# Cross-attention layer on one core: queries turned by DMA and VectorE instead of TensorE, with new written orders

## The chip, the cores and the metric

The kernel runs on one NeuronCore of a Trainium2 chip. The metric is the device time of one execution in microseconds (us); less is better. A measurement of this kernel repeats within about 0.2%.

## What is computed

One transformer block with cross-attention, 16 batches, all in float32: 512 queries of width 256 against 1601 keys, 16 heads of width 16, and an MLP of width 1024.

```python
def _L0_xattn_ref(Q, KV, Wq, bq, Wk, bk, Wv, bv, Wo, bo, W1, b1, W2, b2, ln_q_g, ln_q_b, ln_ff_g, ln_ff_b):
    qn = _layer_norm(Q, ln_q_g, ln_q_b)
    q = (qn @ Wq + bq).reshape(B, Lq, H, DH).transpose(0, 2, 1, 3)
    k = (KV @ Wk + bk).reshape(B, Lkv, H, DH).transpose(0, 2, 1, 3)
    v = (KV @ Wv + bv).reshape(B, Lkv, H, DH).transpose(0, 2, 1, 3)
    scores = jnp.einsum('bhqd,bhkd->bhqk', q, k) / jnp.sqrt(jnp.float32(DH))
    attn = jax.nn.softmax(scores, axis=-1)
    ctx = jnp.einsum('bhqk,bhkd->bhqd', attn, v)
    ctx = ctx.transpose(0, 2, 1, 3).reshape(B, Lq, D)
    x = Q + (ctx @ Wo + bo)
    h = _layer_norm(x, ln_ff_g, ln_ff_b)
    ff = jax.nn.silu(h @ W1 + b1) @ W2 + b2
    return x + ff
```

## The kernel before

The batches run one after the other, and each batch in four quarters of four heads. A quarter q of batch b has 26 pairs of score products (L1324, letter `s`, one per head and half a tile of keys), 26 exponentials on ScalarE (L863, letter `e`), and 13 tiles of products of values with probabilities (L1343, `p`, four 32-column matmuls a tile; a four-byte matmul stands as two records). Softmax subtracts the exact row maximum: score rows with queries on the partitions (L1309, `rows_ps`, letter `m`, 52 a quarter) are made a quarter and more ahead, and VectorE reduces each (L1079, `chunk_max`). Every fourth group of rows holds the last 65 keys: four short matmuls of 65 columns. There are two buffers of `rows_ps`, so TensorE may be two `m` ahead of VectorE. The maxima, negated (letter `n`), go through a small TensorE product (`turn`, L1244), a ScalarE copy and three DMAs of SyncE (`place_shift`, L539) into the last rows of `q_stack`, before the next quarter's scores.

Scores and rows are products of bfloat16 parts: ScalarE writes a projection (`whole`, L824) and its first part (L828), GpSimd the second and third (L641 to L644), and SyncE copies the parts into `k_stack` and `q_stack` (`place`, L455; `repeat_parts`, L464).

All other matmuls are the letter `d`, one `side` bank for all of them: keys (`k`, L1250), values (`v`, L1258), query transposes (`x`, L1248), query projection (`q`, L1254), output projection (`wo`, L1262), transposes of the MLP's input (`h`, L1265), and the MLP (`w1`, L1269; `w2`, L1273). The list `BOTH` says which of them stand in which quarter; the output projection and MLP of batch b-1 and the keys, values and queries of b+1 stand in batch b. In the first and last batch those that have no batch to serve are left out, the letters stay.

The strings `TENSOR`, `SCALAR` and `VECTOR`, one a quarter, are the order on each engine, written out by hand: each letter is one step. They are the same for all 16 batches. SyncE and GpSimd follow their own `quarter` functions in order of the code, and wait there for semaphores; nothing behind a waiting instruction of a queue goes ahead.

The context arrives in chunks of 512 keys through `load_ctx` in blocks of 32 channels, so that VectorE's transpose of 32x32 blocks (`turn_ctx`, L1047, letter `t`) makes the channels-first form `ctxT` of it. The rows of `wk_sb` and `wv_sb` are permuted to fit (`load_rows`). `ctx_blocks` has two halves, used in turn by chunks 0 to 3. The queries go another way: `load_x` (L504) brings x as it is into `x_nat`, VectorE takes moments (`x` in `VECTOR`, in three stages), GpSimd normalises in place (`normalise_x`, L661), TensorE transposes (8 products of 128x128 in two steps), and ScalarE scales and shifts out of the bank into `qnT` (L799).

Of the kernel before, what the change touches and what calls it, by code (L numbers as in the profile page):

```python
# [35 lines left out]
P = 128  # L36
# [30 lines left out]
N_SECOND = 3 + KC * (P // 32)  # L67
# [12 lines left out]
def tiles_in(c):  # L80
# [25 lines left out]
    "pmmssssmddmdddssmmdddssssmmddddssmddmsddmsssmdmddmdmpppmssmsdsmdddmssmdddmsdmsssmddmpmmpmddddmsmsssm"  # L106
    "ddmmddsmsssmppsmmddsmddmsmsssmddddsmmsppdmmdddssssmdmdmssmdmssmsdsmmppp",
    "ssdssmmddmssmssmpmssmssmpmmsssspmdssssmmpppmsssmsmdssmmssdmssmssmdmmppmmssdmssmssmmdmdmmpmddsmssdddd"
    "mmpmddddsssmmdmdmmppsmddddsmssmddmdmddmdmsssmsddmmp",
    "pmmdssmdmssdmsmsdddmmssddmsmsssddmdmdddddmmssssddmdmdpppsmmsssdddmdmdddsdmmsssdmdmsddsmmppmmdssmssmd"  # L110
    "ddmssmddddmmsssdmsmdddmmppddmmssddmmsspppdmdddssmssmdmmssssmdssmmppmmss",
# [15 lines left out]


# [131 lines left out]
def xattn_kernel(nc, x, ctx, wq, bq, wk, bk, wv, bv, wo, bo, w1, b1, w2, b2, gq, cq, gf, cf, out):  # L260
    with ExitStack() as stack:
# [27 lines left out]
        ctx_blocks = sb("ctx_blocks", [P, 2, KC * CHUNK])  # L289
        ctxT = sb("ctxT", [P, KC, BLOCK * BLOCKS])  # L290
# [14 lines left out]
        probs = sb("probs", [P, PROBS, 4 * LQ])  # L305
        o_sb = sb("o_sb", [P, LQ])
# [72 lines left out]
        x_guessed = sem("x_guessed")  # L379
        h_guessed = sem("h_guessed")  # L380
# [1064 lines left out]
```

## Time and profile before

| | |
|---|---|
| median of 3 runs | 3350.74 us (3349.56 to 3351.97) |
| profiled execution | 3350.18 us |
| its span | 3348.4 us |
| TensorE clock granted, mean | 0.989 |
| TensorE / VectorE / ScalarE / GpSimd busy | 98% / 78% / 65% / 29% |

The quarters of a batch in the middle of the run last about 50.3, 49.5, 51.8 and 49.9 us. In this document a quarter of the trace is a stretch between the first TensorE rows of two of them: the second quarter of batch 6 is 1349.0 to 1398.7 us, and the last batch's four quarters begin at 3112.4, 3162.7, 3209.2 and 3257.5 and end at 3297.6. A row of a timeline gives start, length, engine, line, operation and tiles; neighbouring equal instructions are merged, and matmuls overlap in the pipe, so the time that a group takes from TensorE's stream is read from its start to the start of the next row. A row of windows gives the stretch and its length, then busy us and instructions of TensorE's matmuls, its weight loads, VectorE, ScalarE and GpSimd, then the granted clock, the DMA engines' share and GB/s.

### The profile page before, as it was taken

What the parts mean: (1) busy time and instruction counts of PE and PEld (TensorE: products, weight loads), DVE (VectorE), ACT (ScalarE), POOL (GpSimd) and SP (SyncE); (2) the same over time, 40 slices, a digit from 0 to 9 for tenths busy, and PEclk for the clock granted to TensorE, in tenths of its full rate; (3) what the DMA queues carried; (4) which work ended last, traced back from release to release, by engine and by line L of the source; (5) the groups of instructions that cost most, each with busy time, mean ns of one, the idle gap of its engine ahead of it and who ended that gap; (6) DMA issues with size and microseconds to landing.
All of it is one profiled execution on the core that took longest, in us unless ns stands there. A gap on an engine that the chain in (4) does not pass through costs nothing.

```text
span 3348.4 us, 51845 instructions
## 1 busy us (share of the span) xinstructions
PE 3273.7 (98%) x19204; PEld 1598.5 (48%) x19204; DVE 2598.7 (78%) x4771; ACT 2165.4 (65%) x2731; POOL 963.1 (29%) x1312
## 2 busy tenths in 40 slices
PE   6899999999999999999999999999999999999988
PEld 2344444554445455444554445455444554445435
DVE  5778778787887878778787887878778777887762
ACT  1466666666666766667666666766667666666654
POOL 5032324223332332324222332232324213342200
PEclk7899999999999999999999999999999999999998
DMA  5332222322223332222322223331222322222200
GB/s 106 66 54 42 42 48 46 59 53 45 48 42 51 60 59 38 42 51 48 59 53 40 48 46 52 60 59 36 41 52 51 59 53 37 49 45 43 47 7 13
DMA packets 201790, 162.94 MB, mean 49 GB/s; under 512 B 142912, under 2 KB 182848, under 8 KB 198464
## 3 DMA queue, kind: packets, MB, share of 16 engines
q1 hardware_dynamic: 199504, 158.79, 26.4%
q8 instruction: 152, 2.49, 0.3%
q10 hardware_dynamic: 2032, 0.82, 0.1%
q14 instruction: 102, 0.84, 0.1%
HBM read 46.43 MB, written 8.39 MB: 16 GB/s over the span
## 4 chain that ended last, share of the span: by engine, by line
PE 83%; SPq 10%; DVE 3%; DMA 2%; issue 1%; ACT 1%; ACTq 0%; DVEq 0%
PE o_ps L1343 20%; PE rows_ps L1309 19%; PE scores L1324 18%; SPq L455 6%; PE side L1273 6%; PE side L1250 5%; PE side L1269 5%; PE side L1258 4%; SPq L464 3%; DVE chunk_max L1079 2%; PE side L1254 2%; PE side L1262 1%; DMA x_nat<-in_x 1%; SPq L539 1%; PE side L1244 0%
## 5 line engine op out<-in xcount | busy, mean ns | idle before, releaser
L1079 DVE TENSOR_REDUCE chunk_max<-rows_ps 128x1 f32<-128x512 f32 (+1 forms) x3328 | 2109.3, 666 | 602.3 <-PE rows_ps L1309 586.5
L863 ACT ACTIVATE probs<-scores 128x1024 f32<-128x1024 f32 (+1 forms) x1664 | 1633.0, 1020 | 733.2 <-PE scores L1324 615.6
L1309 PE MATMUL rows_ps<-k_stack,q_stack 96*128 96x512 bf16 (+1 forms) x4096 | 1139.8, 337 | 35.9 <-DVE chunk_max L1079 22.0
L1324 PE MATMUL scores<-q_stack,k_stack 99*128 99x512 bf16 (+1 forms) x3328 | 991.0, 380 | 7.2 <-ACT probs L863 5.6
L1343 PE MATMUL o_ps<-probs,v_sb 128*32 128x512 f32 x6656 | 811.1, 602 | 0.2 <-ACT o_sb L852 0.2
L1309 PEld LDWEIGHTS rows_ps<-k_stack,q_stack 96*128 96x128 bf16 x4096 | 342.5, 97 | 675.9 <-DVE chunk_max L1079 438.1
L1324 PEld LDWEIGHTS scores<-q_stack,k_stack 99*128 99x128 bf16 (+1 forms) x3328 | 321.3, 99 | 372.9 <-issue 64.9
L1343 PEld LDWEIGHTS o_ps<-probs,v_sb 128*32 128x32 f32 x6656 | 171.0, 109 | 409.4 <-issue 348.0
L697 POOL TENSOR_TENSOR o_sb<-o_sb,denom 128x512 f32<-128x512 f32 x31 | 39.4, 1271 | 1086.3 <-DVE denom L1065 1086.3
L1269 PE MATMUL side<-hT,w_sb 128*128 128x256 f32 x976 | 268.3, 380 | 0.0
L1273 PE MATMUL side<-w_sb,ffT 128*128 128x256 f32 x960 | 266.7, 381 | 0.2 <-DVE ffT L1012 0.2
L1258 PEld LDWEIGHTS side<-wv_sb,ctxT 128*128 128x128 f32 x1612 | 230.4, 188 | 50.0 <-issue 12.9
L1258 PE MATMUL side<-wv_sb,ctxT 128*128 128x128 f32 x1612 | 236.6, 275 | 0.0
L1269 PEld LDWEIGHTS side<-hT,w_sb 128*128 128x128 f32 x976 | 184.5, 190 | 50.0
L1250 PE MATMUL side<-ctxT,wk_sb 128*128 128x512 f32 x496 | 207.1, 513 | 0.0
L1273 PEld LDWEIGHTS side<-w_sb,ffT 128*128 128x128 f32 x960 | 180.0, 190 | 53.0 <-issue 1.1
L656 POOL TENSOR_TENSOR newton<-rstd 128x2 f32<-128x2 f32 (+1 forms) x138 | 39.7, 287 | 484.1 <-DVE half_var L951 476.9
L695 POOL TENSOR_TENSOR attT<-o_sb,denom 128x512 f32<-128x512 f32 x32 | 42.0, 1312 | 419.6 <-DVE denom L1065 419.6
L641 POOL TENSOR_TENSOR rest<-whole,k_parts 128x512 f32<-128x512 f32 x124 | 117.3, 946 | 157.6 <-ACT k_parts L828 148.6
L834 ACT ACTIVATE ffT<-side,half_b 128x256 f32<-128x256 f32 x240 | 100.7, 472 | 76.1 <-PE side L1269 74.3
L642 POOL TENSOR_TENSOR k_parts<-whole,k_parts 128x512 bf16<-128x512 f32 x124 | 124.1, 1000 | 0.0
L1012 DVE SCALAR_TENSOR_TENSOR ffT<-tanh_sb,ffT 128x512 f32<-128x512 f32 x120 | 105.3, 878 | 23.9 <-ACT tanh_sb L842 23.9
(133 smaller groups left out, 2037.1 us busy)
## 6 DMA issues: line engine op xcount, KB each, us to landing
k_stack<-k_parts SPq DMA_DIRECT2D x768, 50.0 KB, 2.2
k_stack<-k_stack SPq DMA_DIRECT2D x192, 200.1 KB, 5.6
ctx_blocks<-in_ctx SPq DMA_DIRECT2D x188, 128.0 KB, 3.1
q_stack<-q_parts SPq DMA_DIRECT2D x762, 16.0 KB, 1.8
q_stack<-q_stack SPq DMA_DIRECT2D x189, 64.0 KB, 3.4
x_nat<-in_x SPq DMA_DIRECT2D x16, 512.0 KB, 4.0
resid<-in_x SPq DMA_DIRECT2D x32, 256.0 KB, 2.9
out<-resid SPq DMA_DIRECT2D x32, 256.0 KB, 2.3
```

The lines of the kernel that those rows point to most:

```text
L455: queue.dma_start(dst[16 * slot:16 * slot + 16, h, :], src[16 * h:16 * h + 16, part, :])\
L641: seq.inc(nc.gpsimd.tensor_tensor(rest[:, 0:w], src, first, ALU.subtract))
L642: seq.inc(nc.gpsimd.tensor_tensor(second, src, first, ALU.subtract))
L863: nc.scalar.activation(probs[0:rows, probs_of(b, q, t), 2 * LQ * pair:2 * LQ * (pair + 1)], scores[0:rows, 2 * LQ * pair:2 * LQ * (pair + ...
L1079: nc.vector.tensor_reduce(dst, src, AX.X, ALU.max).then_inc(rows_read, 1)
L1250: ins = nc.tensor.matmul(side[:, 0:width(arg)], wk_sb[:, j, P * s:P * (s + 1)], ctxT[:, j, CHUNK * arg:CHUNK * arg + width(arg)], start=(j ...
L1258: ins = nc.tensor.matmul(side[0:rows, P * t:P * (t + 1)], ctxT[:, j, P * i:P * i + rows], wv_sb[:, j, P * s:P * (s + 1)], start=(j == 0), ...
L1269: ins = nc.tensor.matmul(side[:, QH * i:QH * (i + 1)], w1_sb[:, j, P * m:P * (m + 1)], hT_of[hf][:, j, :], start=(j == 0), stop=(j == KC - 1))
L1273: ins = nc.tensor.matmul(side[:, 0:D], ffT_of[hf][:, j, P * t:P * (t + 1)], w2_sb[:, j, :], start=(j == 0), stop=(j == FM - 1))
L1309: last = nc.tensor.matmul(rows_ps[:, m % 2, d0:d0 + w], q_stack[s][0:STACK, h, P * t:P * (t + 1)], k_stack[s][0:STACK, h, k0:k0 + w], star ...
L1324: ins = nc.tensor.matmul(scores[0:keys_in(t), LQ * j:LQ * (j + 1)], k_stack[s][:, h, P * t:P * t + keys_in(t)], q_stack[s][:, h, :], start ...
L1343: last = nc.tensor.matmul(o_ps[32 * j:32 * j + 32, :], v_sb[q // 2][0:rows, t, col:col + 32], probs[0:rows, probs_of(b, q, t), LQ * j:LQ * ...
```

## The change

The queries now go the way of the context. After GpSimd has normalised them in `x_nat`, SyncE moves them in 16 DMAs (`move_x`) into one half of `ctx_blocks`, once chunk 2 of the next context has been turned out of it; VectorE turns them in two transposes (`turn_x`, letter `u`) into `qnT`, and ScalarE scales and shifts in place (`scale_x`, letter `x` of `SCALAR`). The query projection waits for these. `("x", 0)` and `("x", 1)` leave the list `BOTH`; batch 0 alone still transposes on TensorE, from `x_first`, since `wq_sb` has permuted rows now. `load_x` of batch b+2 is issued in the last quarter of batch b, and `load_x(1)` in the prologue. The small loads of `gq` and `cq` move from ScalarE's queue, two, to SyncE's, eight; the load of `wq` becomes eight DMAs.

The order strings are written anew, and the last batch has strings of its own.

```diff
-N_SECOND = 3 + KC * (P // 32)
+N_SECOND = 2 * (P // 32) + 2 * KC * (P // 32)
     [("w1", (0, 3))] + [("k", (0, c)) for c in range(4)]
-    + [("x", 0), ("x", 1), ("q", 0), ("turn", 0), ("w2", (0, 0))],
+    + [("q", 0), ("turn", 0), ("w2", (0, 0))],
 VECTOR = (
...
-    "xmmmmxmmmmttmimmittmmmxmmgmmmmmmmttmmmmmmmtmtmmmmmmmmmnmmmmmmmmmmmmy",
+    "xmmtmmtmmmimmximmxmmmtttmmmmmtmmmmmgmmmmmmmmttmmmmuummmnmmmmmmmmmmmmmym",
...
+TENSOR_LAST = (
...
+        x_blocks = ctx_blocks[:, 0, :]
+        x_first = probs[:, 1, 0:QT * D].rearrange("p (t d) -> p t d", d=D)
...
                     sp.wait_ge(ctx_turned, (b * NCH + c - 1) * KC)
+                    if c == 0:
+                        wait(sp, x_turned, (b - 1) * KC)
...
+            def move_x(b):
+
+                sp.wait_ge(xn_ready, b + 1)
+
+                sp.wait_ge(ctx_turned, (b * NCH + 3) * KC)
+                for p in range(P // BLOCK):
+                    for a in range(P // BLOCK):
+                        sp.dma_start(x_blocks[BLOCK * p:BLOCK * (p + 1), :]
+                                     .rearrange("r (t a i) -> r t a i", t=QT, i=RUN)[:, :, a, :],
+                                     x_nat[BLOCK * a:BLOCK * (a + 1), :, RUN * p:RUN * (p + 1)]).then_inc(x_moved, 16)
...
+                for dst, src in ((gq_c, gq), (cq_c, cq)):
+                    for p in range(P // BLOCK):
+                        with nc.allow_non_contiguous_dma(reason="a bias, once"):
+                            sp.dma_start(dst[BLOCK * p:BLOCK * (p + 1), :],
+                                         src[RUN * p:RUN * (p + 1)].rearrange("(k i) -> i k", k=KC))\
+                                .then_inc(loaded_second, 16)
...
+                load_x(1)
...
-                    load_x(b + 1)
                     for c in (2, 3):
 
                         load_ctx(b + 1, c)
+                    move_x(b + 1)
...
+                    sp.wait_ge(x_moved, (b + 1) * (16 * (P // BLOCK) ** 2))
+                    load_x(b + 2)
...
-                normalise(x_nat, x_nat, QT, xn_ready)
+                normalise(x_nat, x_first if isinstance(b, int) and b == 0 else x_nat, QT, xn_ready)
...
+            def scale_x(b, kc):
+
+                act.wait_ge(x_turned, (b - 1) * KC + (kc + 1))
+                nc.scalar.activation(qnT[:, kc, :], qnT[:, kc, :], ACT.Identity, bias=cq_c[:, kc:kc + 1],
+                                     scale=gq_c[:, kc:kc + 1]).then_inc(qn_made, 1)
...
-                for dst, src in ((gq_c, gq), (cq_c, cq)):
-                    column(act, dst, src, KC, loaded_second)
-                act.dma_start(wq_sb[:, :, :], wq.rearrange("(c p) n -> p c n", p=P)).then_inc(loaded_second, 16)
+                load_rows(act, wq_sb, wq, loaded_second)
...
+            def turn_x(b, kc):
+
+                if kc == 0:
+                    dve.wait_ge(x_moved, b * (16 * (P // BLOCK) ** 2))
+                nc.vector.transpose(qnT[:, kc, :].rearrange("p (j r) -> p j r", r=BLOCK),
+                                    x_blocks.rearrange("p (j k i) -> p j k i", k=KC, i=BLOCK)[:, :, kc, :])\
+                    .then_inc(x_turned, 1)
...
+                    elif kind == "q" and s == 0:
+
+                        wait(pe, qn_made, b * KC)
...
-                for what in TENSOR[q]:
+                for what in (TENSOR_LAST if isinstance(b, int) and b == B - 1 else TENSOR)[q]:
```

Three places where the strings move instructions. First TensorE in the second quarter of batch 6, around the query projection; L1248, L1254, L1309, L1324, L1343 and L1244 of before are L1327, L1333, L1388, L1403, L1422 and L1323 of the changed kernel. Before:

```order
2542 L1324 MATMUL scores<-q_stack,k_stack 128x512 x2
2543 L1248 MATMUL side<-ident,x_nat 128x128 x4
2544 L1309 MATMUL rows_ps<-k_stack,q_stack 128x512 x2
2545 L1343 MATMUL o_ps<-probs,v_sb 32x512 x4
2546 L1309 MATMUL rows_ps<-k_stack,q_stack 128x512
2547 L1248 MATMUL side<-ident,x_nat 128x128 x4
2548 L1324 MATMUL scores<-q_stack,k_stack 128x512 x3
2549 L1309 MATMUL rows_ps<-k_stack,q_stack 128x512 x2
2550 L1254 MATMUL side<-qnT,wq_sb 128x512
2551 L1309 MATMUL rows_ps<-k_stack,q_stack 128x65 x4
2552 L1254 MATMUL side<-qnT,wq_sb 128x512
```

The same place in the changed kernel:

```order
2572 L1422 MATMUL o_ps<-probs,v_sb 32x512 x12
2573 L1388 MATMUL rows_ps<-k_stack,q_stack 128x512
2574 L1403 MATMUL scores<-q_stack,k_stack 128x512 x2
2575 L1388 MATMUL rows_ps<-k_stack,q_stack 128x512
2576 L1403 MATMUL scores<-q_stack,k_stack 128x512 x2
2577 L1388 MATMUL rows_ps<-k_stack,q_stack 128x65 x4
2578 L1333 MATMUL side<-qnT,wq_sb 128x512
2579 L1388 MATMUL rows_ps<-k_stack,q_stack 128x512
2580 L1333 MATMUL side<-qnT,wq_sb 128x512
```

The two groups of transposes are gone, and value products stand in one run of three tiles ahead of the projection.

Second, VectorE in the same quarter (`x_nat` moments, then chunk maxima with the turning of context between them). Before, the last four turnings of the context and what follows:

```order
823 L1079 TENSOR_REDUCE chunk_max<-rows_ps 128x1 x7
824 L1047 STREAM_TRANSPOSE ctxT<-ctx_blocks 128x512 x2
825 L1079 TENSOR_REDUCE chunk_max<-rows_ps 128x1 x3
826 L1079 TENSOR_REDUCE chunk_max<-rows_ps 128x4
827 L1079 TENSOR_REDUCE chunk_max<-rows_ps 128x1 x3
828 L1047 STREAM_TRANSPOSE ctxT<-ctx_blocks 128x96
829 L1079 TENSOR_REDUCE chunk_max<-rows_ps 128x1
830 L1047 STREAM_TRANSPOSE ctxT<-ctx_blocks 128x96
831 L1079 TENSOR_REDUCE chunk_max<-rows_ps 128x1 x8
```

In the changed kernel, from the third pair of context turnings to the queries:

```order
840 L1111 STREAM_TRANSPOSE ctxT<-ctx_blocks 128x512 x3
841 L1151 TENSOR_REDUCE chunk_max<-rows_ps 128x1 x5
842 L1111 STREAM_TRANSPOSE ctxT<-ctx_blocks 128x512
843 L1151 TENSOR_REDUCE chunk_max<-rows_ps 128x1 x5
844 L1076 SCALAR_TENSOR_TENSOR ffT<-tanh_sb,ffT 128x512
845 L1151 TENSOR_REDUCE chunk_max<-rows_ps 128x1 x2
846 L1151 TENSOR_REDUCE chunk_max<-rows_ps 128x4
847 L1151 TENSOR_REDUCE chunk_max<-rows_ps 128x1 x5
848 L1111 STREAM_TRANSPOSE ctxT<-ctx_blocks 128x96 x2
849 L1151 TENSOR_REDUCE chunk_max<-rows_ps 128x1 x4
850 L1119 STREAM_TRANSPOSE qnT<-ctx_blocks 128x512 x2
```

The third pair of context turnings ends behind the 19th maximum of the quarter, and the two new transposes stand behind the 36th.

Third, TensorE at the start of the last batch's fourth quarter, where no score rows are left. Before:

```order
6269 L1324 MATMUL scores<-q_stack,k_stack 128x512 x5
6270 L1343 MATMUL o_ps<-probs,v_sb 32x512 x4
6271 L1324 MATMUL scores<-q_stack,k_stack 128x512 x3
6272 L1269 MATMUL side<-hT,w_sb 128x256 x2
6273 L1324 MATMUL scores<-q_stack,k_stack 128x512 x2
```

In the changed kernel:

```order
6316 L1422 MATMUL o_ps<-probs,v_sb 32x512 x8
6317 L1403 MATMUL scores<-q_stack,k_stack 128x512 x10
6318 L1422 MATMUL o_ps<-probs,v_sb 32x512 x8
6319 L1403 MATMUL scores<-q_stack,k_stack 128x512 x3
6320 L1348 MATMUL side<-hT,w_sb 128x256
```

Ten score products stand in a row, where there were five and then a tile of value products. (A four-byte product is one row here and two records in the trace.)

## Rows read from the trace of the kernel before

**Rows 1.** The page: busy us, share of the span, instructions.
```profile
PE 3273.7 (98%) x19204; PEld 1598.5 (48%) x19204; DVE 2598.7 (78%) x4771; ACT 2165.4 (65%) x2731; POOL 963.1 (29%) x1312
```

**Rows 2.** The page: the chain that ended last, by line.
```profile
PE o_ps L1343 20%; PE rows_ps L1309 19%; PE scores L1324 18%; SPq L455 6%; PE side L1273 6%; PE side L1250 5%; PE side L1269 5%; PE side L1258 4%; SPq L464 3%; DVE chunk_max L1079 2%; PE side L1254 2%; PE side L1262 1%; DMA x_nat<-in_x 1%; SPq L539 1%; PE side L1244 0%
```

**Rows 3.** Windows: first batch, batches 1 to 14, last batch.
```profile
84.60:290.30 205.70, 189.08 (x1064) 73.03 (x1068) 156.90 (x286) 121.98 (x143) 44.61 (x53) 0.95 0.29 50
290.30:3112.40 2822.10, 2819.06 (x16804) 1394.07 (x16800) 2262.66 (x4131) 1892.75 (x2380) 845.90 (x1176) 1.00 0.27 49
3112.40:3297.60 185.20, 174.40 (x1024) 77.72 (x1020) 111.67 (x206) 119.56 (x143) 25.41 (x40) 0.98 0.13 26
```

**Rows 4.** Waits of TensorE, 400 to 3110 us: total, times, longest.
```profile
PE rows_ps L1309 <- DVE chunk_max L1079: 1.9, 4, 0.6
```

**Rows 5.** Windows: second quarter of batch 6.
```profile
1349.00:1398.70 49.70, 49.39 (x280) 21.05 (x280) 41.46 (x82) 34.78 (x44) 28.45 (x41) 1.00 0.08 19
```

**Rows 6.** Timeline of TensorE around the query transposes, batch 6.
```profile
1382.07 0.61 PE L1248 MATMUL side<-ident,x_nat 128*128 128x128 f32 x4
1382.51 0.60 PE L1309 MATMUL rows_ps<-k_stack,q_stack 96*128 96x512 bf16 x2
1383.04 1.07 PE L1343 MATMUL o_ps<-probs,v_sb 128*32 128x512 f32 x8
1384.04 0.39 PE L1309 MATMUL rows_ps<-k_stack,q_stack 96*128 96x512 bf16 x1
1384.27 0.60 PE L1248 MATMUL side<-ident,x_nat 128*128 128x128 f32 x4
```

**Rows 7.** Timeline of TensorE at a run of two tiles.
```profile
1422.97 1.92 PE L1343 MATMUL o_ps<-probs,v_sb 128*32 128x512 f32 x16
1424.83 0.51 PE L1309 MATMUL rows_ps<-k_stack,q_stack 96*128 96x65 bf16 x5
```

**Rows 8.** Timeline of TensorE at short rows and MLP products.
```profile
1474.91 0.60 PE L1273 MATMUL side<-w_sb,ffT 128*128 128x256 f32 x2
1475.35 0.28 PE L1309 MATMUL rows_ps<-k_stack,q_stack 96*128 96x65 bf16 x4
1475.47 0.68 PE L1273 MATMUL side<-w_sb,ffT 128*128 128x256 f32 x2
1475.98 0.38 PE L1309 MATMUL rows_ps<-k_stack,q_stack 96*128 96x512 bf16 x1
```

**Rows 9.** Waits of all engines over the span.
```profile
DVE stats L936 <- DMA x_nat<-in_x: 23.5, 16, 3.0
```

**Rows 10.** Timeline of VectorE, second quarter of batch 6.
```profile
1372.88 1.29 DVE L1047 STREAM_TRANSPOSE ctxT<-ctx_blocks 128x512 f32<-128x512 f32 x2
```

**Rows 11.** Timeline of ScalarE, same quarter.
```profile
1385.59 1.93 ACT L863 ACTIVATE probs<-scores 128x1024 f32<-128x1024 f32 x2
```

**Rows 12.** Timeline of GpSimd, same quarter.
```profile
1365.73 0.20 POOL L656 TENSOR_TENSOR newton<-rstd 128x4 f32<-128x4 f32 x1 [2.67 <-DVE half_var L951]
...
1369.70 4.85 POOL L661 TENSOR_SCALAR x_nat<-x_nat,moments,rstd 128x256 f32<-128x256 f32 x4
```

**Rows 13.** Timeline of SyncE's queue, third quarter of batch 6.
```profile
1396.66 7.53 SPq L455 DMA_DIRECT2D k_stack<-k_parts  x12
...
1422.74 3.76 SPq L464 DMA_DIRECT2D q_stack<-q_stack  x3
```

**Rows 14.** The page: DMA issues, count, KB each, median us to landing.
```profile
k_stack<-k_parts SPq DMA_DIRECT2D x768, 50.0 KB, 2.2
...
ctx_blocks<-in_ctx SPq DMA_DIRECT2D x188, 128.0 KB, 3.1
```

**Rows 15.** Timeline of the opening, all engines.
```profile
14.64 3.57 SPq L477 DMA_DIRECT2D wv_sb<-in_L_xattn_Wv  x8
...
24.66 7.58 SPq L455 DMA_DIRECT2D k_stack<-k_parts  x12
...
45.79 1.01 PE L1309 MATMUL rows_ps<-k_stack,q_stack 96*128 96x512 bf16 x2 [12.47 <-DMA q_stack<-q_stack]
```

More of the change, by code:

```diff
@@ L105 @@
 TENSOR = (
[L106 to L111, printed above, removed]
@@ L660, in normalise @@
                 for n in range(tiles):
-                    last = nc.gpsimd.tensor_scalar(dst[:, n, :], src[:, n, :], moments[:, first + n, 0:1],
+                    to, of = dst[:, n, :], src[:, n, :]
+                    if dst is x_first:
+                        to, of = to.rearrange("q (k p c) -> q p k c", k=KC, c=BLOCK), of.rearrange(
+                            "q (p k c) -> q p k c", k=KC, c=BLOCK)
+                    last = nc.gpsimd.tensor_scalar(to, of, moments[:, first + n, 0:1],
                                                    rstd[:, first + n:first + n + 1],
@@ L747, in quarter @@
                         add_mlp_bias(b - 1, hf)
-                if ("x", 0) in kinds:
+                if q == 1 and not (isinstance(b, int) and b == B - 1):
                     normalise_x(b + 1)
@@ L896, in quarter @@
             def quarter(b, q, start, steps):
-                unit, reads = iter(range(UNITS)), iter(chosen(q, steps, ("v", "k", "q", "x", "turn", "h", "w1")))
-                for what in SCALAR[q]:
+                unit, reads, turned = iter(range(UNITS)), iter(chosen(q, steps, ("v", "k", "q", "turn", "h", "w1"))), \
+                    itertools.count()
+                for what in (SCALAR_LAST if isinstance(b, int) and b == B - 1 else SCALAR)[q]:
                     if what == "c":
@@ L904, in quarter @@
                             copy_group(b - 1, 3)
+                    elif what == "x":
+                        if b < B - 1:
+                            scale_x(b + 1, next(turned))
                     elif what == "r":
@@ L1127, in quarter @@
                 row, stage, x_stage, turn = itertools.count(), iter(range(2)), iter(range(STAGES)), itertools.count()
+                turn_of_x = itertools.count()
                 silus, sums, adds = (iter(chosen(q, steps, (kind,))) for kind in ("w1", "wo", "w2"))
                 moment = itertools.product(chosen(q, steps, ("wo",)), range(STAGES))
-                for what in VECTOR[q]:
+                for what in (VECTOR_LAST if isinstance(b, int) and b == B - 1 else VECTOR)[q]:
                     if what == "m":
@@ L1146, in quarter @@
                             x_moments(b + 1, next(x_stage))
+                    elif what == "u":
+                        if b < B - 1:
+                            turn_x(b + 1, next(turn_of_x))
                     elif what == "t":
@@ L1247, in side_product @@
                 elif kind == "x":
-                    ins = nc.tensor.transpose(side[:, P * i:P * (i + 1)], x_nat[:, i, P * arg:P * (arg + 1)], ident[:, :])
+                    ins = nc.tensor.transpose(side[:, P * i:P * (i + 1)], x_first[:, i, P * arg:P * (arg + 1)], ident[:, :])
                 elif kind == "k":
```

49 lines of the change are left out of this document (40 added, 9 removed).

## The prediction, made before the changed kernel ran

> **What bounds the kernel now.** Read first which engine is full, then whether it ever waits, and only then what its instructions cost. The page's busy times give TensorE 98% of the span, VectorE 78%, ScalarE 65% [rows 1], and in the chain that ended last three quarters of the time are matmul lines [rows 2]. The chain also holds 9% of SyncE's queue, so the issuing of DMAs can matter. The windows by stage tell where TensorE is really full: over batches 1 to 14 (290.3 to 3112.4 us) it is busy 2819.06 of 2822.10 us at a granted clock of 1.00, 201.6 us a batch; over the first batch it is busy 189.08 of 205.7, over the last 174.40 of 185.2, and in both the clock is a little lower [rows 3]. In the 14 batches TensorE's waits come to almost nothing [rows 4]. So in them a microsecond taken from TensorE's stream is a microsecond of the kernel, as long as no new wait appears; VectorE is the engine nearest to becoming one, with 41.46 of 49.70 us busy in the second quarter, where this change adds to it [rows 5].
>
> **What leaves TensorE in a batch.** Three terms.
>
> The transposes of the queries: 8 of them, in two groups of 4. The row of four is 0.61 long but overlaps the next; what counts is from its start to the start of the next row, 1382.07 to 1382.51, 0.44 for four, 0.11 each [rows 6]. 8 x 0.11 = 0.88 us. The Trainium skill (TensorE: Matmul & The Clock Gate, Part 4: PE-mode transpose) gives about 275 ns for a 128x128 transpose within a kernel; by that the term would be 2.2 us.
>
> The value products with probabilities (L1343, 4 matmuls as 8 records for one tile of keys). A run of one tile takes 1.00 (1383.04 to 1384.04), a run of two 1.86 (1422.97 to 1424.83), so a tile is 0.86 and a run has 0.14 of its own; the two rows before it take 0.53 instead of 0.44 (1382.51 to 1383.04), another 0.10 [rows 6, 7]. So each separate run costs 0.24. By the order tables a batch had 28 runs and has 27 (first and last quarter joined): 0.24 us. The row's extra agrees with the Trainium skill (TensorEngine Tiling (Array Packing), Key Properties), which says that a change of tiling mode drains TensorE; it gives no size.
>
> Four-byte products straight behind the short 65-wide rows. The pair at 1474.91 takes 0.44, the pair at 1475.47, behind the four short rows, 0.51 [rows 8]. The tables before put a side product behind short rows in seven places a batch, now in three, and of these one is new in kind (a value projection): 4 x 0.07 = 0.3 us.
>
> Sum 0.88 + 0.24 + 0.3 = 1.4 us a batch, over 14 batches 20 us. Further, the load of the queries now goes out half a batch earlier; before, VectorE's first step of the second quarter waited for it each time, 23.5 us in 16 waits [rows 9], and part of that reached TensorE: of the 3.0 us idle in 14 batches I take 2 away [rows 3, 4]. The first batch loses its 8 transposes too, 0.9.
>
> **What comes in, and what hides it.** VectorE gets two transposes, priced by the same shape on the key side: 1.29 us for two [rows 10]. 41.5 + 1.3 = 42.8 of a quarter that shrinks to about 48.5, 88%. ScalarE's two reads out of PSUM become two of the same size in place: nothing. GpSimd does the same work, earlier. The price of VectorE's two lies between 0 (hidden) and 14 x 1.3 = 18 us (all on the path). Its steps stand next to product rows that TensorE buffers by two, and today the same load shows 1.9 us of wait in all 14 batches [rows 4]; I take another 2.
>
> SyncE gets 16 DMAs, and these are the dangerous part, since TensorE's query projection now stands behind this chain: GpSimd's normalised queries, 16 issues, landing, two VectorE transposes, ScalarE's scaling, TensorE. I walk it with 0 at the quarter's first row. The third moments step stands behind 11 chunk maxima. With 0.22 for a 512-wide row (1384.04 to 1384.27) [rows 6], 0.43 for a four-byte one (two records of half the width take 0.44 [rows 8]) and the prices above, TensorE reaches maximum 11 at 9.7; VectorE, behind its reciprocal steps, finishes the third step at about 12.2. GpSimd took 8.8 from the start of its Newton steps to the end of normalising (1365.73 to 1374.55) [rows 12]: 21.1. The third pair of key chunks is turned after maximum 19, at 20.3, so GpSimd's end decides. An SBUF to SBUF issue is 0.63 (7.53 for 12) [rows 13], so 16 take 10.0 and the last starts at 30.5. A small SBUF piece lands 2.2 after its issue, the large 256-byte loads of keys 3.1 [rows 14]: landed 32.7 to 33.6. VectorE comes to its turn behind maximum 36, at about 34. TensorE notices only from about 35 (third maximum after it) and the projection, at 38.0, needs both scalings, which end near 36.7. So there is a margin of 1.4 to 2.3 us; cost zero, and 1 us for each us beyond, 15 times. Behind the DMAs on SyncE stand the shift rows of the next quarter (wanted from 42) and then the stack filling: both later than 31, no cost.
>
> The opening: the eight small loads of scale and offset now stand on SyncE ahead of the value weights (14.64 to 18.21), at the 0.45 of those loads 3.6 us [rows 15]. TensorE's opening transposes wait for all of them, and so at most 3.6 later than before. But the first score rows (45.79) hang on the last placings of query parts, and half of these stand on SyncE behind 12 placings of keys, 24.66 to 32.24 [rows 15], which are not moved: these cover most of the lateness. Bounds 0 and 3.6; I take 0.7, near the cover.
>
> The last batch: of its 185.2 us 10.8 are idle, and 3 to 4 more lie in the clock of 0.98 [rows 3]. The change writes new orders for it. The order fence shows the fourth quarter opening with ten score products in a row, five exponentials at about 1 us each (1.93 for two) [rows 11] against 2.2 us of TensorE's work, which is no better than the old opening; the second quarter spreads its maxima better. Runs of value products go from 28 to 30, +0.5. Bounds: 12 won, 5 lost; I take 1 won, close to the old row, since the fence shows no clear gain.
>
> **Sum.** 20 + 2 + 0.9 + 1 - 2 - 0.7 = 21.2 us less. The profiled execution is 3350.18 (span 3348.4 and 1.8 around it); the median of the runs is 0.6 above it. 3350.2 - 21.2 + 0.5 = 3329.5 us.
>
> **Rivals.**
> 1. The last batch's orders carry much of its idle time away: 12 instead of 1, 3318 us. For it: 10.8 us idle and lowered clock. Against: the work per quarter is as before and its opening is bare of filler. Chance 0.12.
> 2. VectorE becomes the bound in the second quarter: three quarters of its 1.3 us appear, 1 us in each of 14 batches, with half of the small terms lost: 3350 - 21 + 14 + 2 = 3345 us. For it: 88% busy. Against: it waits for TensorE often even now. Chance 0.12.
> 3. Slower: the moved queries come late. Between stacks, in SBUF too, an issue takes 1.25 (3.76 for 3) [rows 13]. At that price 16 take 20, land at 43.3, and TensorE stands 8 us in each of 15 batches: 3329 + 120 = 3449. It decides from 0.77 us an issue (margin 2.3 used up), and makes the kernel slower than before from about 0.86. Against: those DMAs move 64 KB each, these 32 KB, as 128 pieces of 256 bytes. The Trainium skill (DMA: Bandwidth & Descriptors, Specifications) speaks against such pieces, below 512 bytes; the key loads, of the same pieces, land in 3.1 nonetheless. Chance 0.08.
> 4. A transpose costs TensorE its whole record, 0.61 - 3 x 0.11 = 0.28 [rows 6], since the pipe has to empty around it: 8 x 0.17 x 15 = 20 more, 3310 us. Against: the next row begins 0.44 after the first of the four. The Trainium skill's 275 ns (page named above) would mean this case. Chance 0.03.
>
> The forecast's own case has 0.65, from 3320 to 3338.
>
> **How the numbers follow.** The range leaves out rival 3, rival 4 and the ends of the others: 3314 to 3346. What a measurement of this kernel can tell from no change is 0.2%, 6.7 us, so faster means under 3344. Faster: forecast, rivals 1 and 4, and a third of rival 2, 0.84. Same: two thirds of rival 2, 0.08. Slower 0.08.
>
> **What would show it.** Right: TensorE busy again over 99.8% of batches 1 to 14 and 200.1 us a batch; the turning of the queries on VectorE has no wait for a landing ahead of it, or one under 1 us; the second quarter of a batch about 1.1 shorter, the others within 0.5 of before. Wrong: a wait of VectorE for the moved queries over 2 us, or of TensorE for the scaled ones; score rows of the second quarter waiting for chunk maxima; a last batch far from 185 us.

## The result and the profile after

The changed kernel takes 3324.75 us (median of 4 executions, 3318.19 to 3325.59), the one before 3350.69 (4 executions, 3349.56 to 3351.97). The ratio is 0.9912 with a 95% interval of 0.9900 to 0.9925, so it is faster by 26 us, 0.9%. In five rounds on another chip it was 0.9906 (0.9892 to 0.9921). The forecast was 3329.5, range 3314 to 3346. The profiled execution took 3324.14 with a span of 3322.3.

The page of after, busy us and then the chain that ended last by line, answers to [rows 1, 2]:

```profile
PE 3251.8 (98%) x19084; PEld 1603.3 (48%) x19084; DVE 2592.7 (78%) x4801; ACT 2175.1 (65%) x2731; POOL 955.3 (29%) x1312
...
PE o_ps L1422 23%; PE rows_ps L1388 22%; PE scores L1403 21%; PE side L1348 6%; PE side L1352 6%; PE side L1337 5%; PE side L1329 5%; PE side L1333 2%; PE side L1341 2%; SPq L485 1%; DVE chunk_max L1151 1%; PE side L1323 1%; SPq L528 0%; SPq L494 0%; PE side L1344 0%
```

TensorE is full as before, with 120 matmuls fewer (15 batches of 8 transposes). By engine, SyncE's queue has 3% of this chain, where it had 10% of the chain before. The windows of after (columns: stretch, us, busy PE, PEld, DVE, ACT, POOL, granted clock, DMA share, GB/s) show the first batch, batches 1 to 14, the second quarter of batch 6 and the last batch, in answer to [rows 3, 5]:

```profile
85.40:295.00 209.60, 192.91 (x1052) 74.13 (x1056) 157.40 (x288) 123.18 (x143) 44.57 (x53) 0.93 0.31 54
...
295.00:3091.40 2796.40, 2796.39 (x16696) 1399.10 (x16692) 2258.36 (x4158) 1900.67 (x2380) 837.44 (x1176) 1.00 0.29 52
1344.10:1392.40 48.30, 48.30 (x272) 20.40 (x268) 41.56 (x80) 35.12 (x44) 27.53 (x39) 1.00 0.15 28
3091.40:3271.70 180.30, 172.88 (x1028) 76.71 (x1024) 109.56 (x205) 119.94 (x143) 24.08 (x39) 0.99 0.14 26
```

Over batches 1 to 14 TensorE is busy 2796.39 of 2796.40 us. The 26 us are made of these (us, by the start of each quarter's first matmul in the two traces):

| part | before | after | difference | forecast |
|---|---|---|---|---|
| start of the first quarter | 84.6 | 85.4 | +0.8 | +0.7 |
| batch 0 | 205.6 | 209.6 | +4.0 | -0.9 |
| batches 1 to 14 | 2822.2 | 2796.3 | -25.8 | -20 |
| last batch | 185.2 | 180.3 | -4.9 | -1 |

The four quarters of batches 1 to 14 took 50.29, 49.26 to 50.36, 51.77 and 49.92 before, and 50.28, 48.24, 51.81 and 49.39 after, nearly the same in every batch. So two things are in the 25.8: 1.52 us a batch, 21.3 in all, between the undisturbed quarters (forecast 1.42, 20), and 4.7 that came and went with the landing of the queries, of which 0.3 is left after, so 4.4. By quarter the 1.52 are 0.01, 1.02, -0.04 and 0.53. The wait of [rows 9] is one wait now, in the opening:

```profile
DVE stats L1000 <- DMA x_nat<-in_x: 1.9, 1, 1.9
```

The new chain of the queries, in the second quarter of batch 6, which starts at 1344.1 (timeline of all engines; columns: start, us, engine, line, operation, number):

```profile
1359.60 4.85 POOL L717 TENSOR_SCALAR x_nat<-x_nat,moments,rstd 128x256 f32<-128x256 f32 x4
...
1364.71 10.39 SPq L545 DMA_DIRECT2D ctx_blocks<-x_nat  x16
...
1378.37 1.29 DVE L1119 STREAM_TRANSPOSE qnT<-ctx_blocks 128x512 f32<-128x512 f32 x2
...
1379.40 1.52 ACT L906 ACTIVATE qnT<-qnT,cq_c,gq_c 128x512 f32<-128x512 f32 x2
...
1382.24 0.67 PE L1333 MATMUL side<-qnT,wq_sb 128*128 128x512 f32 x1
```

Counted from 1344.1 the queries are normalised at 20.4 (walked in the prediction: 21.1), the last issue ends at 31.0 (31.1), VectorE turns at 34.3 (34), and the projection starts at 38.1 (38.0). An issue costs 0.65 here, not 1.25. This batch is one of the quick ones: over batches 1 to 14 the 16 issues take 10.4 to 11.2 us, and the last move lands 32.2 to 33.1 into the quarter (walked: 32.7 to 33.6). VectorE has no wait ahead of the turns in any batch.

### The profile page after: what moved, and what is told of

The parts are those of the page before. It is cut to its first block, busy times and chain, and to the rows that moved or that the text cites. A ratio compares the mean times of both kernels' runs of the same rounds, so it can differ in the third digit from the quotient of the medians.

```text
span 3322.3 us, 51902 instructions
## 1 busy us (share of the span) xinstructions
PE 3251.8 (98%) x19084; PEld 1603.3 (48%) x19084; DVE 2592.7 (78%) x4801; ACT 2175.1 (65%) x2731; POOL 955.3 (29%) x1312
## 4 chain that ended last, share of the span: by engine, by line
PE 94%; SPq 3%; DVE 2%; ACT 1%; issue 0%; DMA 0%; ACTq 0%; DVEq 0%
PE o_ps L1422 23%; PE rows_ps L1388 22%; PE scores L1403 21%; PE side L1348 6%; PE side L1352 6%; PE side L1337 5%; PE side L1329 5%; PE side L1333 2%; PE side L1341 2%; SPq L485 1%; DVE chunk_max L1151 1%; PE side L1323 1%; SPq L528 0%; SPq L494 0%; PE side L1344 0%
## 5 line engine op out<-in xcount | busy, mean ns | idle before, releaser
L1388 PE MATMUL rows_ps<-k_stack,q_stack 96*128 96x512 bf16 (+1 forms) x4096 | 1152.9, 337 | 29.5 <-DVE chunk_max L1151 16.9
L1403 PE MATMUL scores<-q_stack,k_stack 99*128 99x512 bf16 (+1 forms) x3328 | 990.0, 380 | 7.4 <-ACT probs L925 4.2
L1422 PE MATMUL o_ps<-probs,v_sb 128*32 128x512 f32 x6656 | 809.0, 602 | 0.2 <-ACT probs L925 0.2
L1388 PEld LDWEIGHTS rows_ps<-k_stack,q_stack 96*128 96x128 bf16 x4096 | 336.3, 97 | 675.6 <-DVE chunk_max L1151 352.7
L1403 PEld LDWEIGHTS scores<-q_stack,k_stack 99*128 99x128 bf16 (+1 forms) x3328 | 321.6, 100 | 337.4 <-issue 39.6
L1422 PEld LDWEIGHTS o_ps<-probs,v_sb 128*32 128x32 f32 x6656 | 171.9, 109 | 393.3 <-issue 304.2
L1337 PEld LDWEIGHTS side<-wv_sb,ctxT 128*128 128x128 f32 x1612 | 240.5, 188 | 39.5 <-ACT shift_parts L853 0.7
L1337 PE MATMUL side<-wv_sb,ctxT 128*128 128x128 f32 x1612 | 247.3, 276 | 0.0
L865 ACT COPY v_sb<-side 128x512 f32<-128x512 f32 x124 | 62.5, 504 | 85.7 <-PE side L1337 83.1
L696 POOL TENSOR_TENSOR k_parts<-rest,k_parts 128x512 bf16<-128x512 f32 x124 | 111.1, 896 | 9.7
```

Of the source, the lines that this page charges most:

```text
L696: nc.gpsimd.tensor_tensor(parts[:, 2, off:off + w], rest[:, 0:w], second, ALU.subtract).then_inc(split, 1)
L1337: ins = nc.tensor.matmul(side[0:rows, P * t:P * (t + 1)], ctxT[:, j, P * i:P * i + rows], wv_sb[:, j, P * s:P * (s + 1)], start=(j == 0), ...
L1388: last = nc.tensor.matmul(rows_ps[:, m % 2, d0:d0 + w], q_stack[s][0:STACK, h, P * t:P * (t + 1)], k_stack[s][0:STACK, h, k0:k0 + w], star ...
L1403: ins = nc.tensor.matmul(scores[0:keys_in(t), LQ * j:LQ * (j + 1)], k_stack[s][:, h, P * t:P * t + keys_in(t)], q_stack[s][:, h, :], start ...
L1422: last = nc.tensor.matmul(o_ps[32 * j:32 * j + 32, :], v_sb[q // 2][0:rows, t, col:col + 32], probs[0:rows, probs_of(b, q, t), LQ * j:LQ * ...
```

## The experiments

Letters: `p` a tile of value products, `m` product rows, `s` scores, `d` a side product. Runs marked b start from the kernel before, those marked a from the changed one. Each of the first ten was one profiled execution, read by quarters, since TensorE's undisturbed quarters repeat to 0.02 us while the opening, batch 0 and the last batch together differ by several us between traces with equal orders there; the last two were timed in five rounds. The totals, which for this reason settle little, were (us):

| run | total | kernel before, same chip |
|---|---|---|
| b_xload_runs, b_x_twice, b_short_rows, a_old_orders | 3356.32, 3364.14, 3357.89, 3418.95 | 3357.53 |
| a_last_plain, a_turns_twice, a_moves_20, a_moves_24 | 3323.57, 3322.25, 3323.71, 3377.93 | 3358.05 |
| a_first_q1, a_first_all | 3324.15, 3328.01 | 3348.62 |
| a_again, a_rows_placed | 3323.34, 3319.48 | 3353.45 |

**b_xload_runs: the load of the queries early, and two runs joined.**

```
+ load_x(1)                      # end of the prologue
- load_x(b + 1)                  # second quarter of b
+ load_x(b + 2)                  # last quarter of b
first quarter:  ...ddm pmmp mdddd...   ->  ...ddm mmpp mdddd...
fourth quarter: ...ssss mpmmp       ->  ...ssss mmmpp
```

> The kernel before with two edits that act in different quarters. (1) The load of the queries is issued half a batch earlier, as in the changed kernel; nothing else of the queries' path is touched. My theory as the traces now read: the second quarters, 49.26 to 50.36 us before, all become 49.26, which is 4.7 us in sum; the prediction's term had 2 us; a rival says that the wait was VectorE's alone and gives nothing. (2) In the first and the fourth quarter one run of value products is joined to its neighbour (the tile stands two rows later). Theory: 0.24 us less in each of these quarters (50.29 to 50.05, 49.92 to 49.68), 6.7 us over 14 batches. Rival: the entry into a run is hidden behind the rows, no change. Total by theory 3339 us, by both rivals 3350.

All 14 second quarters took 49.26, where before they took 49.26 to 50.36. The 4.7 are the load's, and the wait is TensorE's in the end. How much it costs differs: in b_short_rows, with the late load, the excess over the shortest second quarter is 0.2 in 14 batches, in b_x_twice 4.2. These are different kernels with one trace each, so chance and their orders are not told apart. This term is a spread taken away rather than a fixed gain.

The joined runs went the other way: first quarter 50.79 for 50.29, fourth 50.42 for 49.92. The timeline of TensorE in the first quarter shows it:

```profile
1322.77 0.90 PE L1310 MATMUL rows_ps<-k_stack,q_stack 96*128 96x512 bf16 x2
1323.94 0.39 PE L1310 MATMUL rows_ps<-k_stack,q_stack 96*128 96x512 bf16 x1 [0.27 <-DVE chunk_max L1080]
1324.26 1.92 PE L1344 MATMUL o_ps<-probs,v_sb 128*32 128x512 f32 x16
```

The edit left three rows in a row. From 1322.77 to the start of the value products are 1.49 us, where three rows and the 0.10 ahead of a run need 0.75: 0.74 of waiting for VectorE's maxima, of which only 0.27 shows as idle time. The quarter is longer by 0.50, so the joining did give 0.24, and its place cost 0.74. The 0.24 is confirmed only in this indirect way.

**b_x_twice: each transpose of the queries on TensorE issued twice.**

```
- "x": (QT, 1)
+ "x": (QT, 2)        # and 8 letters d more in the second quarter
```

> The kernel before, with each transpose of the queries on TensorE issued twice in a row, so 16 in a batch instead of 8. It prices the disputed term alone. Theory: 0.11 us each, the second quarter 0.88 us longer (49.26 to 50.14 at its shortest), 13 to 14 us in all, 3364 us. Rival 4 of the prediction: 0.28 each, 2.2 us a batch, 3384 us (the 275 ns of the Trainium skill, TensorE: Matmul & The Clock Gate, Part 4: PE-mode transpose, would give the same).

The second quarter is 50.13 at its shortest (49.26 before): 8 transposes more are 0.87 us, 0.11 each. The timeline of TensorE has eight in a row from 1388.83 to 1389.71, 0.88:

```profile
1388.83 1.04 PE L1248 MATMUL side<-ident,x_nat 128*128 128x128 f32 x8
1389.71 0.60 PE L1309 MATMUL rows_ps<-k_stack,q_stack 96*128 96x512 bf16 x2
```

Rival 4, that a transpose costs its whole record, falls. Batches 1 to 14 took 11.8 us more than in the trace of before; the total is only 6.6 over the kernel before on that chip, whose trace is not kept. The 275 ns of the Trainium skill (TensorE: Matmul & The Clock Gate, Part 4: PE-mode transpose) do not hold for a transpose's place in a full stream; they are near the length of its record, 1.04 less seven times 0.11.

**b_short_rows: 65-wide rows moved behind the side products.**

```
first quarter:  smdmddmdmppp -> smdmdddmmppp;  mmpmddddmsm -> mmpddddmmsm;  msssmddddsmm -> msssddddmsmm
fourth quarter: mdsssmsdmdmssm -> mdsssmsddmmssm;  ssssdmdmsdmdsdss -> ssssdmdmsddmsdss
```

> The kernel before, with five of its seven 65-wide row groups that stood ahead of a four-byte side product moved behind it: three in the first quarter, two in the fourth. Theory: 0.07 us at each place, the first quarter 50.29 to 50.08, the fourth 49.92 to 49.78, 4.9 us in all, 3345.3 us. Rival: the 0.07 only moves to what stands behind the rows now, no change.

The fourth quarter became 49.81, 0.11 for two places. The first became 51.17, 0.88 longer. Its rows now meet other rows, and VectorE is behind at four places. At this one the row at 1327.09 stands 0.47 behind the start of the score, where the step is 0.22:

```profile
1326.28 0.50 PE L1309 MATMUL rows_ps<-k_stack,q_stack 96*128 96x65 bf16 x5
1326.62 0.38 PE L1324 MATMUL scores<-q_stack,k_stack 99*128 99x512 bf16 x1
1327.09 0.39 PE L1309 MATMUL rows_ps<-k_stack,q_stack 96*128 96x512 bf16 x1
```

So the term is real and small (0.055 a place here), and again the place of a row counts for more.

**a_old_orders: the new way, the old orders.**

```
TENSOR = before's, less the 8 letters of the transposes
SCALAR = before's, two r of the transposes left out, xx ahead of the projection's read
VECTOR = before's, uu behind the 36th m of the second quarter
```

> The changed kernel's way of moving and turning the queries, with the orders of the kernel before: TensorE's letters less the 8 transposes, the two turns on VectorE behind its 36th maximum of the second quarter, the two scalings on ScalarE where its reads were, and no orders of its own for the last batch. Theory: GpSimd's normalised queries are ready 24 to 25 us into the second quarter, the 16 moves take 10.4 more and land at 37 to 38, the turns and scalings end at 41 to 42, and the query projection, wanted at 35.6, stands 5 to 6 us in each batch: second quarter 53 to 55 us, 3395 to 3420 us in all. Rival: the orders matter little, the wait is under 1 us, period about 200.7 us, 3333 us.

3418.95 us, where the kernel before took 3357.53 on that chip, one execution each, so 61 more; the second quarters took 53.7 to 56.0, on average 54.5. The waits of VectorE, then of TensorE (total us, times, longest):

```profile
DVE qnT L1119 <- DMA ctx_blocks<-x_nat: 38.7, 14, 3.6
...
PE rows_ps L1388 <- DVE chunk_max L1151: 46.5, 14, 4.1
```

Here is the slower side of the forecast: without the orders the mechanism loses. But the waits of TensorE explain only 3.3 of the 6.2 us a batch (54.5 against 49.26 less 0.88). Most of the rest is the clock. Two windows of the second quarter of batch 6, the first with TensorE's wait in it:

```profile
1407.00:1411.00 4.00, 1.75 (x13) 0.41 (x5) 0.91 (x2) 1.94 (x2) 2.50 (x5) 0.99 0.18 33
1411.00:1417.60 6.60, 5.21 (x11) 1.77 (x11) 4.46 (x14) 2.09 (x3) 0.00 (x0) 0.50 0.00 0
```

TensorE stood from about 1408.7 and the granted clock is at its lower level (1.2 GHz) from 1411 for 6.6 us, which costs up to 3.3 more. Each of the 14 batches has such a stretch, seven of 3.4 us and seven of 6.8, which at half the clock is 2.6 a batch on average.

**a_last_plain: no orders of its own for the last batch.**

```
- (TENSOR_LAST if isinstance(b, int) and b == B - 1 else TENSOR)[q]
+ TENSOR[q]                       # SCALAR and VECTOR likewise
```

> The changed kernel, with the orders of batches 1 to 14 used for the last batch too. The last batch took 185.2 us before and 180.3 with orders of its own; in three other runs of the old orders it took 182.2 to 184.7, by how long the clock was at its lower level there. Theory: the orders themselves are worth about 2 us, the rest of the 4.9 was the clock; the last batch comes out at 182 to 185 us, with second quarter 46 to 47. Rival: all of 4.9 is the orders', 185 or more. Everything else unchanged, 3324 plus 2 to 5 us.

The last batch took 180.36 us against 180.3, both with one short stretch of lower clock in the last quarter; its quarters are 50.28, 44.91, 46.17, 39.0 for 50.35, 45.21, 45.54, 39.19. So the orders written for it are worth nothing that can be seen beside orders that are new anyway, against the rival and against my theory of 2. What shortens the last batch is that its orders are new at all, common or its own: by some 3.5 at the same clock (182.16 us with the old ones where no stretch fell into it, in b_xload_runs with the 0.5 of its edit taken off, and 178.66 with the new ones in a_turns_twice). The new way of the queries has no part in it: in a_old_orders, which has the way with the old orders, the second and third quarters are 46.45 and 46.67, as in b_xload_runs, against 45.22 and 45.54. The rest is the clock, 0.96 in two quarters before and in one after.

**a_turns_twice: each turn on VectorE issued twice.**

```
+ link(nc.vector.transpose(...the same...))   # ahead of each transpose of turn_x
```

> The changed kernel, with each of VectorE's two transposes of the queries issued twice, so 1.3 us more work on VectorE in each second quarter at the same place. Rival 2 of the prediction said that VectorE's steps there show. By the trace the maximum behind the turns starts at 1379.59 in batch 6 and TensorE's next row starts at 1380.81: 0.5 us of cover is left when 0.65 for the maximum is counted. Theory: of the 1.3 to 1.5 added 0.6 to 0.9 shows in each second quarter (48.24 to 48.9 or 49.1), about 11 us in all. If nothing shows, VectorE had slack; if all of it, the prediction's zero for the first turns was luck.

The second quarter went from 48.24 to 48.57: 0.33 of the 1.4 us added, less than the 0.6 to 0.9 of my theory. TensorE's wait in batches 1 to 14:

```profile
PE rows_ps L1390 <- DVE chunk_max L1153: 2.2, 14, 0.2
```

So VectorE's steps there have about 1.1 us of cover. The likely reason is the run of three tiles of value products (2.7 us without a row), under which the orders put the turns; a kernel with the run elsewhere was not made. Rival 2 falls. My 2 us of new waits were too many: in the changed kernel the view of TensorE's waits over batches 1 to 14 is empty.

**a_moves_20 and a_moves_24: 4 or 8 of the 16 moves split in two.**

```
+ for t in ((0, 2), (2, 4)) if p * (P // BLOCK) + a < MORE else ((0, 4),):
      sp.dma_start(...[:, t[0]:t[1], a, :], x_nat[..., t[0]:t[1], ...])
```

> The changed kernel, with 4 of the 16 moves of queries split in two (20 DMAs, the same bytes). At 0.65 us an issue the last lands 2.6 us later. Rival 3 of the prediction gave a margin of 1.4 to 2.3 us. Theory: landed about 1379.3 in batch 6 where VectorE now comes at 1378.37, so VectorE waits about 1 us and TensorE 0.3 to 0.6 in each second quarter (48.24 to 48.7), 4 to 8 us in all. If smaller pieces issue faster, nothing shows.

> As the one with 20 moves, with 8 of the 16 split (24 DMAs), 5.2 us more of issuing. Theory: VectorE waits 3 to 4 us for the landing, TensorE 2.5 to 3.3 in each second quarter (51 to 52 us), and the clock falls now and then behind that wait, as it did with the old orders, so 3365 to 3385 us. Rival: the wait hits only VectorE, which has slack, under 1 us a batch, 3335.

In batch 6 issuing takes 14.09 us for 20 and 16.05 for 24, after 10.39 for 16; on average over batches 1 to 14 it is 13.5, 16.0 and 10.7, at the shortest 0.65 an issue in all three. The waits over batches 1 to 14, with 20:

```profile
DVE qnT L1122 <- DMA ctx_blocks<-x_nat: 19.0, 14, 2.6
...
PE rows_ps L1391 <- DVE chunk_max L1154: 4.0, 7, 1.3
```

and with 24:

```profile
DVE qnT L1122 <- DMA ctx_blocks<-x_nat: 51.1, 14, 4.5
...
PE rows_ps L1391 <- DVE chunk_max L1154: 33.8, 14, 3.2
```

With 20, on average 2.8 us more of issuing, VectorE waits 1.4 on average and the 14 second quarters are 5.9 us longer in all. With 24, 5.3 us more, it waits 3.7 and they are 53.5 longer; total 3377.93. The landings give VectorE's margin directly: in the changed kernel the last move lands at 32.2 to 33.1, VectorE comes to it at 34.2, so 1.0 to 2.0 us, 1.6 on average. TensorE has about 1.1 more: in batch 1 with 20 moves VectorE waits 2.38 and the quarter is 1.30 longer, in batch 8 it waits 2.59 and the quarter is 1.52 longer. That makes 2.1 to 3.1 us, 2.7 on average, before a later landing costs anything. Rival 3 had 1.4 to 2.3 for this, and by the same walk 0.4 to 1.3 for VectorE, so the true margins were larger.

The loss past the margin is steeper than 1 for 1: the 53.5 are for the most part 33.8 and 1.8 of waits (the second one for shift rows, in batch 8) and nine stretches of 3.4 us at the lower clock, which cost about 15. With waits of up to 1.3 us (20 moves) the clock stayed at its higher level (2.4 GHz) in all 14 batches.

**a_first_q1 and a_first_all: batch 0 with rows spread.** In batch 0 the steps of the MLP are absent, so the changed second quarter, written `...dmdmdmdmdmdmdmdm`, ends there in eight rows in a row. The timeline of TensorE in after:

```profile
193.43 0.39 PE L1388 MATMUL rows_ps<-k_stack,q_stack 96*128 96x512 bf16 x1 [0.26 <-DVE chunk_max L1151]
194.03 0.39 PE L1388 MATMUL rows_ps<-k_stack,q_stack 96*128 96x512 bf16 x1 [0.21 <-DVE chunk_max L1151]
194.63 0.39 PE L1388 MATMUL rows_ps<-k_stack,q_stack 96*128 96x512 bf16 x1 [0.21 <-DVE chunk_max L1151]
...
196.42 1.21 PE L1388 MATMUL rows_ps<-k_stack,q_stack 96*128 96x512 bf16 x2 [0.21 <-DVE chunk_max L1151]
```

The window behind it in after:

```profile
196.20:209.80 13.60, 13.03 (x42) 4.92 (x42) 7.73 (x13) 5.12 (x5) 0.00 (x0) 0.50 0.27 54
```

and the kernel before at the same place:

```profile
197.00:210.00 13.00, 12.43 (x82) 5.33 (x78) 10.26 (x18) 7.19 (x9) 0.00 (x0) 1.00 0.30 58
```

42 matmuls against 82 in about 13 us: the clock is at its lower level, 1.2 GHz, and the third quarter takes 52.8 us for 47.8. With the changed orders batch 0's third quarter was 51.7 to 52.9 in each of seven traces; with the old ones it was 47.8 in all five, a_old_orders among them, which has the moves too. (Another stretch, near 150 us, comes in some traces of either kind.)

```
TENSOR_FIRST[1] = ...smmppsmssmsmdmmmdmsmmpmddmddsmssdddddddd   # batch 0 only
```

> The changed kernel, with one letter string more: in the second quarter of batch 0 alone TensorE's product rows are spread by VectorE's work, so that the quarter no longer ends in eight rows in a row, each 0.60 us behind the last. In all five runs of the changed orders so far a stretch at the lower clock follows that tail (at 185 to 199 us) and batch 0's third quarter takes 51.7 to 52.9 us, where it took 47.8 with the old orders. Theory: the clock falls because TensorE is paced by VectorE there; with the rows spread the third quarter takes 45 to 47 us and batch 0 loses 5 to 8 us. Rival: the stretch has another cause and stays, batch 0 as before within 1 us. A stretch near 148 us, which comes in some runs and not in others, can hide or add 4 us in the second quarter.

> The same for all four quarters of batch 0. The first quarter (57.6 us for 44.0 of TensorE's work) has its rows ahead of VectorE at several places too. Theory: every quarter comes closer to its work (44.0, 42.7, 44.9, 39.1 by durations in the trace): 52 to 56, 46 to 50, 45 to 47, 42 to 45, batch 0 in 185 to 198 instead of 205 to 210. Rival: the new rows wait for their placed parts instead, and nothing is won beyond the third quarter's 6.

a_first_q1: the window of the lower clock comes later and is half as long, and the third quarter takes 50.38 instead of 52.8:

```profile
203.20:209.80 6.60, 6.24 (x15) 1.78 (x14) 4.52 (x7) 3.97 (x4) 0.00 (x0) 0.50 0.42 78
```

So the order of the rows moves the fall, but rows spread evenly make TensorE wait elsewhere (for exponentials, 1.3 us at the end of the quarter); batch 0 took 210.9, and 213.4 with all four quarters spread. Neither is a gain on the 209.6 of the changed kernel, and the 5 to 8 us of the first theory and the 185 to 198 of the second are not there. What exactly makes the clock fall in batch 0 stays open: VectorE paces TensorE through all of it.

**a_again and a_rows_placed: the changed kernel once more, and its TensorE letters placed anew.** For the second, the letters of batches 1 to 14 were moved by adding up the steps on each engine (0.217 a row, 0.605 a maximum, 0.24 a run, 0.08 behind 65-wide rows, and about 0.1 for a four-byte product straight behind a value run, 0.32 instead of 0.22 in the changed kernel's trace). ScalarE's and VectorE's letters are the same.

```
+ TENSOR_MID = ( "pmmddddddddssmmssdddmssmddmss...", ...)
- TENSOR_LAST if isinstance(b, int) and b == B - 1 else TENSOR
+ TENSOR_LAST if b == B - 1 else TENSOR if b == 0 else TENSOR_MID
```

> The changed kernel itself, timed in five rounds beside the one before, on the same chip as the next run. Theory: batches 1 to 14 again 199.74 us each, batch 0 between 204.8 and 209.6 by whether the stretch of lower clock near 148 us comes, the last batch 178.7 or 180.3; so 3318 to 3326 us, and 0.988 to 0.992 of the kernel before.

> The changed kernel with TensorE's letters of batches 1 to 14 placed anew; ScalarE, VectorE, batch 0 and the last batch as they are. As many runs of value products (27), but no four-byte product straight behind one (there were 2), one behind 65-wide rows (there were 3), and no third row in a row where VectorE is behind. By the steps in the traces (0.298 against 0.218 behind 65-wide rows; 0.413 against 0.322 behind a value run) that is 0.16 and 0.18 us a batch, and small differences of 0.001 to 0.002 a product may bring as much again. Theory: 199.74 becomes 199.2 to 199.4, 5 to 7 us less than the changed kernel, 3312 to 3320. Rival: rows land where VectorE has no time for them, a wait appears in some quarter, no gain or a loss.

a_again: 3323.34 us (3318.16 to 3324.42), before on that chip 3353.45. a_rows_placed: 3319.48 (3315.60 to 3321.03), ratio to before 0.9899 (0.9883 to 0.9916). Its window over batches 1 to 14:

```profile
293.90:3084.00 2790.10, 2788.75 (x16692) 1395.76 (x16688) 2235.61 (x4158) 1890.48 (x2380) 836.52 (x1176) 1.00 0.29 52
```

2790.1 for 2796.4, 6.3 us, as expected; the second and fourth quarters are 0.11 and 0.28 shorter, the third 0.02 longer. The first is 0.20 shorter at its shortest but varies now, 50.08 to 50.81, and is 0.06 shorter on average; the trace names a wait of 0.7 for the shift rows and one of 0.3 for exponentials. The gain is that of the whole placing: which of its moves brought how much was not tried. The medians differ by 3.9 us, and the two intervals against before overlap: by the traces it is the better kernel, by the times alone that is likely and not certain.

## Why the prediction was right, and where it was off

**The steady term.** 1.42 us a batch forecast, 1.52 measured. Its largest part, 0.11 for a transpose, was measured by itself (0.87 for 8). The 0.24 of a run shows indirectly, the 0.07 behind 65-wide rows was 0.055 in the one quarter that could be read alone; how the rest of the 1.52 divides between these two was not measured, nor were the new orders run with the old way of the queries, so what they would give alone is known only by these terms. Reading the price off start to start, not off the length of a record, was the step that carried the forecast.

**The load's term was mis-sized**: 2 forecast, 4.7 measured. The step that failed took the idle time of TensorE in the window of [rows 3] as the upper end; the waits of VectorE had passed on into matmuls that stood longer without showing as idle, and the quarters' lengths (49.26 to 50.36) would have shown it. [rows 4] moreover begins at 400 us and leaves out the longest of the waits, 0.9 at 344.1. The size is not a steady one, 0.2 to 4.7 in the three traces with the old orders, the late load and TensorE's transposes.

**What comes in was mis-sized**: 2 forecast, 0 measured. a_turns_twice shows why: even 1.4 us more cost 0.33.

**The moves** went as walked, to within 0.8 us at every step: the queries were normalised 0.7 early, issuing took 0.4 longer or more. Rival 3 was the right danger: a_old_orders and a_moves_24 are both slower than the kernel before. Its margin of 1.4 to 2.3 us was too small, it is 2.1 to 3.1; its price past the margin, 1 us for 1, was too small as well, since it left out the clock.

**The last batch was mis-sized**: 1 forecast, 4.9 measured, and the reason was wrong too. The orders of its own give nothing over the new common ones; new orders of either kind give about 3.5, the clock the rest. The prediction took the order fence to show no clear gain. Rival 1's 12 are not there.

**Batch 0 had the wrong sign**: 0.9 less forecast, 4.0 more measured. The failed step counts only the 8 transposes that leave. The first two quarters together are indeed 0.9 shorter, though their scatter of some 5 us between traces makes that no proof; the third is 5.0 longer. The new second quarter puts rows and MLP products in turn at its end; in batch 0 the products are absent, the rows stand alone, VectorE paces them, and a stretch at 1.2 GHz follows. The order table of batch 0 would have shown the eight rows. How long batch 0 takes varies: 204.8 to 209.8 in seven traces with the changed orders (the two a_first kernels aside), 202.0 to 208.3 in four of the kernel before and its variants.

**The opening** was 0.7 forecast and 0.8 measured, and that match is luck: the first quarter began between 84.6 and 85.9 us in the ten traces with the changed kernel's opening, and between 84.6 and 87.7 in the four of the kernel before and its variants.

**The sum.** The forecast was 4.8 too long. Roughly: 2 us of new waits, 2.4 of the load (4.4 for 2), 3.9 of the last batch and 1.4 of the steady term made it too long, and 4.9 of batch 0 too short. So the mechanism of batches 1 to 14 was right, and that the total came as near as 4.8 is in part luck, errors of 9.7 one way and 4.9 the other.

**The signs.** Those named for "right" came: TensorE without idle time over batches 1 to 14, 199.7 us a batch, no wait ahead of the turns, the second quarter 1.02 shorter; the fourth moved by 0.53, just over the 0.5 allowed. Of those for "wrong" one came, a last batch 4.9 from 185. A reading that nothing hung on: the matmul lines of [rows 2] add up to 81%, not three quarters.

## What to carry to other kernels

Price an instruction that leaves a full engine by the step from its start to the start of the next kind, and check that price by issuing it twice. When work leaves the full engine by way of a chain of other engines, walk the chain to its last step, and write the order so that the chain's start comes early and its end falls under a stretch in which the full engine needs nothing: the same mechanism was 61 us slower than before with the old orders and 26 faster with new ones. In an order shared by a first, a middle and a last round, write out what is left of it where steps are absent.

## What the runs showed of the hardware

Waits of TensorE could cost more than their length, since the granted clock then fell to 1.2 GHz. In a_old_orders each of 14 waits of 3.1 to 4.1 us had a stretch at 0.50 with it, of 3.4 or 6.8 us. In a_moves_24 the eight waits for maxima of 2.4 to 3.2 us had one of 3.4 us each, the six of 1.8 to 2.3 had none; but behind a wait of 1.8 for the shift rows (at 1770.9, batch 8) one came too, and behind one of 2.0 in batch 1 of a_again none. The length of the wait alone does not decide it. A row of matmuls that VectorE spaces at 0.60 us, without a wait over 0.3, was followed by such a stretch as well (0.50 from 196.2 in after).

Moves within SBUF, each of 128 pieces of 256 bytes, cost SyncE 0.65 us an issue, hardly more than the 0.63 of [rows 13], and landed 1.9 us behind it at the median. Splitting some of them in two made the halves no cheaper to issue: at the shortest 10.4, 12.9 and 15.5 us for 16, 20 and 24.
